# Messages split into a high and a low float32r part, the merge made of float32r products, and a reordered prologue

## The chip, the core and the metric

The kernel runs on one NeuronCore of a Trainium2 chip. The number that counts is the device time of one execution, in microseconds (us). The kernel before has a median of 1049.14 us over three runs (1049.01 to 1050.68).

## The reference

One GNN layer over N = 50000 nodes of D = 128 features and E = 25000 edges, sorted by destination:

```
h    = relu(layernorm(x))                       # without scale and shift
xn   = layernorm(h, g1, b1)
msg  = relu(xn[src] + edge_attr)                # 25000 x 128
aggr = segment_sum(msg, dst, num_segments=N)
z    = (1 + eps_gin) * xn + aggr
x2   = h + relu(z @ Wg1 + bg1) @ Wg2 + bg2
out  = x + x2 + gelu(layernorm(x2, g2, b2) @ Wf1 + bf1) @ Wf2 + bf2      # Wf1: 128 x 512
```

All tensors are float32.

## The kernel before, in words

**Tiles.** Nodes are worked on in 98 blocks of 512 rows (128 partitions x J = 4 rows of 128), edges in 49 chunks of 512 (the same shape). Every engine has its own program, and each walks through the same software pipeline by calling a `step(node, edge, halves, apart)` function; `node(o)` and `edge(o)` give the block or chunk that entered the pipeline o steps ago. With the sorted edges of this input all go through `edges_beside_nodes` (L98 in the profile's numbering): 105 node steps t = 0 to 104, and beside them one chunk every two steps. A chunk's step has two halves: odd t does half 0, even t half 1. Ahead of that, in the prologue, `first_chunks` runs three whole edge steps with no nodes beside them, and `half_chunk` the first half of a fourth (so chunk 3 enters there, and chunk 0 is three steps old). Inside a step the order of instructions of each engine is written out by hand; engines wait for each other on semaphores.

**A chunk's way.** GpSimd (POOL) gathers the source rows of x by indirect DMA into `e_x` (L436). VectorE (DVE) takes statistics (`stats`, L675), ScalarE (ACT) makes `e_relu` (L611), DVE takes its statistics, POOL the power -1/2 of the variance (L501, or, from the fifth chunk on, in one instruction with a node's, L456). DVE scales (`e_zg`, L770), adds b1 to the attributes (`add_b1`, L746) and makes `e_sum` (L792). ACT takes the relu, `e_msg` (L581). Where rows of one partition share a destination they are merged with matmuls: DVE compares destinations into `e_match` (L730, four instructions), and TensorE (PE) multiplies `e_match` with `e_msg` into `p_merged` (L938), six float32 products of 128 columns a chunk.
**A block's way.** DVE: statistics, `n_zg` (L831), `n_in` (L848: needs POOL's power `n_rstd`, L456, and the sums `n_aggr` that SyncE's queue reads back), `n_x2` (L802, opens a step), the out-seed `p_out` (L839), `n_z2T_low` (L689), `n_out` (L826). PE: transposes `p_in` (L927) and `p_z2` (L905), `p_g` (L897), `p_gout` (L912), the first feed-forward product `p_f` (L883) and the second `p_out` (L920).
**Order in the steps that the change touches.** DVE, odd t: `n_x2`, node statistics, `n_out`, `n_zg`, `p_out` seed, `n_in`, then `first_half` (chunk statistics, relu statistics, the small e_ columns, `z2_low`, the four `e_match`, `variance_of`), then `add_b1`. DVE, even t: the same node work, then `second_half` (chunk relu statistics, `e_zg`, `e_index`, `z2_low`, `variance_of`, `e_sum`). PE merges a chunk at the end of odd steps, behind `p_in`. In the prologue POOL does, per step, the power of the chunk two steps old, then the gathers of the new one. ACT does `merged_rows` of chunk 0 in step t = 0.

Of the kernel before, what the change touches and what calls it, by code (L numbers as in the profile page):

```python
# [5 lines left out]
ALU = mybir.AluOpType  # L6
# [4 lines left out]
F32R = mybir.dt.float32r  # L11
BF16 = mybir.dt.bfloat16

P = 128
J = 4
# [96 lines left out]
def gnn_kernel(nc, x, edge_attr, edge_cols, dst_rows, g1, b1, g2, b2, eps_gin,  # L112
# [25 lines left out]
    with ExitStack() as ctx:  # L138
# [9 lines left out]
        def ring_sems(name, depth):  # L148
# [37 lines left out]
        e_x, e_attr, e_relu, e_zg, e_attrb, e_sum, e_msg, e_merged = (  # L186
            sb(f"e_{n}", [P, 3, J, D]) for n in ("x", "attr", "relu", "zg", "attrb", "sum", "msg", "merged"))
# [4 lines left out]
        e_match = sb("e_match", [P, 3, J // PAIR, PAIR * (PAIR + 1) // 2, P])  # L192
# [32 lines left out]
         s_ezg, s_eattrb, s_esum, s_emsg, s_ematch, s_eextra, s_eindex, s_emm, s_emerged) = (  # L225
            sem(f"s_e{n}") for n in (
                "copy", "stat", "minus", "relu", "var0", "statu", "var", "rstd",
                "zg", "attrb", "sum", "msg", "match", "extra", "index", "mm", "merged"))
# [42 lines left out]
        def joined(c, apart):  # L271

            return not apart and c.k >= FIRST_JOINED

# [132 lines left out]
        def _(pool):  # L407
# [51 lines left out]

            def merged_first(edge, apart):  # L460
# [16 lines left out]
            def step(node, edge, halves, apart):  # L477
# [20 lines left out]
                if 0 in halves and (c := edge(2)) is not None and not joined(c, apart):  # L498
                    r, s = c.rows, c.slot(3)
                    pool.wait_ge(s_evar, c.at + 1)  # L500
                    nc.gpsimd.tensor_tensor(e_rstd[0:r, s], e_var[0:r, s, 1], minus_half[0:r, 0:J],  # L501
                                            ALU.pow).then_inc(s_erstd, 1)
                if 0 in halves and (c := edge(0)) is not None:
                    gather(c, range(0, PAIR))
                if 1 in halves and 0 in halves:
                    merged_first(edge, apart)
# [8 lines left out]
        def _(act):  # L515
# [34 lines left out]
            def step(node, edge, halves, apart):  # L550
# [14 lines left out]
                if 1 in halves and 0 not in halves:  # L565
                    merged_rows(edge(3))
# [11 lines left out]
                if 0 in halves and (c := edge(3)) is not None:  # L578
                    act.wait_ge(s_esum, c.at + 1)
                    reached(act, s_emm, c.at - 2)  # L580
                    nc.scalar.activation(e_msg[0:c.rows, c.slot(3)], e_sum[0:c.rows, c.slot(3)],  # L581
# [6 lines left out]
                if 0 in halves and 1 in halves:  # L588
                    merged_rows(edge(3))
# [11 lines left out]
                if (b := node(2)) is not None:  # L601
# [3 lines left out]
                                         ACT.Identity).then_inc(s_inT, 1)  # L605
                if 0 in halves and (c := edge(1)) is not None:
# [18 lines left out]
        def _(dve):  # L625
# [80 lines left out]
            def first_half(c, node):  # L706
# [6 lines left out]
                if c is not None:  # L713
# [5 lines left out]
                                            ALU.mult, ALU.add).then_inc(s_evar0, 1)  # L719
                z2_low(node)  # L720
# [15 lines left out]
                variance_of(node)  # L736

# [258 lines left out]
```

## Time and profile before

| | |
|---|---|
| median of three runs | 1049.14 us |
| the profiled execution: its time, its span | 1047.92 us, 1046.2 us |
| mean granted TensorE clock | 0.984 of full |
| busy share PE / PEld / DVE / ACT / POOL | 94 / 82 / 92 / 82 / 79 % |
| DMA | 156.87 MB, mean 150 GB/s |

Busy time is the union of the instructions' intervals; two instructions that follow each other overlap in it (the next starts before the last one's recorded end), so what an instruction costs on a full engine is the distance from its start to the next start, which is shorter than its duration. The three fullest engines are close together, so the question in every stretch is which one sets the pace.

### The profile page before, as it was taken

Reading aid. Unit: us, or ns where it says so; the run is one execution under the profiler, and the core shown is the slowest. Engines: PE = TensorE matmul, PEld = TensorE weight load, DVE = VectorE, ACT = ScalarE, POOL = GpSimd, SP = SyncE. Lnnn points to the kernel's source line nnn. Section 1 sums busy time; section 2 is a strip of 40 time slices with the busy share of each in tenths; the row PEclk is TensorE's granted clock in tenths of the full one; section 3 lists DMA queues with packets and bytes.
Section 4 is the critical chain, followed back from the end, with each engine's and each line's share of the span. In section 5 each row is a group of like instructions: output and inputs, shape, how many; then the busy total and the mean of one; then the engine's idle time right before and its main releaser. Section 6 shows DMA issues by size and latency. Waiting matters only on the chain. (4 is left out here: it accounts for less than half of the span.)

```text
span 1046.2 us, 23086 instructions
## 1 busy us (share of the span) xinstructions
PE 978.5 (94%) x6684; PEld 853.8 (82%) x6684; DVE 965.6 (92%) x3499; ACT 853.2 (82%) x2158; POOL 823.1 (79%) x510
## 2 busy tenths in 40 slices
PE   0359999999999999999999999999999999999978
PEld 0347888888889888888888888888888888888867
DVE  5789999999999999999999999999999999998732
ACT  1358988988888988888888888888888888988853
POOL 6788888888788888888888888888888888876610
PEclk9679999999999999999999999999999999999999
DMA  7765766877785654565565555554564554443221
GB/s 258 211 180 129 217 171 179 240 227 237 233 254 158 152 138 116 138 142 124 136 146 126 139 142 125 139 144 123 139 146 122 139 146 120 116 112 80 52 60 41
DMA packets 110468, 156.87 MB, mean 150 GB/s; under 512 B 24835, under 2 KB 50607, under 8 KB 110334
## 3 DMA queue, kind: packets, MB, share of 16 engines
q1 hardware_dynamic: 70358, 128.99, 38.9%
q0 software_dynamic: 37760, 25.66, 17.5%
q8 instruction: 56, 0.92, 0.4%
q10 hardware_dynamic: 2216, 0.66, 0.3%
q14 instruction: 78, 0.64, 0.2%
HBM read 90.61 MB, written 64.61 MB: 148 GB/s over the span
## 5 line engine op out<-in xcount | busy, mean ns | idle before, releaser
L447 POOL DMA_INDIRECT aggr_sums<-e_merged,e_index x196 | 337.8, 1724 | 81.4 <-issue 71.9
L920 PE MATMUL p_out<-wf,n_act 128*128 128x128 f32 x3136 | 370.4, 276 | 1.8 <-DVE p_out L839 0.2
L920 PEld LDWEIGHTS p_out<-wf,n_act 128*128 128x128 f32 x3136 | 357.7, 191 | 7.1 <-DVE p_out L839 6.2
L456 POOL TENSOR_TENSOR n_rstd<-n_var,minus_half 128x16 f32<-128x16 f32 (+3 forms) x102 | 259.3, 2554 | 52.6 <-DVE n_var L819 32.1
L522 ACT ACTIVATE n_act<-p_f,bf1e_col 128x512 f32<-128x512 f32 x392 | 256.2, 680 | 35.4 <-PE p_f L883 28.9
L436 POOL DMA_INDIRECT e_x<-in_x,e_cols x196 | 222.0, 1133 | 60.2 <-issue 59.2
L883 PE MATMUL p_f<-n_z2T_high,wf_low 128*128 128x512 f32 x392 | 203.3, 519 | 5.7 <-DVE n_z2T_low L689 5.3
L883 PE MATMUL p_f<-n_z2T_high,wf_high 128*128 128x512 f32 x392 | 155.4, 397 | 0.0
L883 PE MATMUL p_f<-n_z2T_low,wf_high 128*128 128x512 f32 x392 | 155.0, 395 | 0.0
L675 DVE BATCH_NORM_STATS2 n_stat<-n_x 128x6 f32<-128x256 f32 x392 | 140.1, 417 | 0.1
L604 ACT ACTIVATE n_inT<-p_in 128x512 f32<-128x512 f32 x98 | 58.5, 597 | 99.5 <-PE p_in L927 87.5
L848 DVE SCALAR_TENSOR_TENSOR n_in<-n_zg,n_rstd,n_aggr 128x128 f32<-128x128 f32 x392 | 111.2, 344 | 24.2 <-DMA n_aggr<-aggr_sums 18.7
L536 ACT ACTIVATE p_gout<-n_relu,n_rstd 128x128 f32<-128x128 f32 x392 | 128.9, 366 | 4.8 <-DVE n_x L802 3.8
L572 ACT ACTIVATE n_relu<-n_x,n_minus 128x128 f32<-128x128 f32 x392 | 124.7, 397 | 8.7 <-DVE n_minus L813 4.6
L598 ACT ACTIVATE n_z<-n_x,n_rstd 128x128 f32<-128x128 f32 x392 | 125.7, 408 | 4.1 <-POOL n_rstd L456 4.1
L883 PEld LDWEIGHTS p_f<-n_z2T_high,wf_low 128*128 128x128 f32 x392 | 74.4, 190 | 50.3 <-ACT n_act L522 22.2
L912 PE MATMUL p_gout<-wg,n_gT 128*128 128x128 f32 (+1 forms) x784 | 106.8, 280 | 8.7 <-ACT p_gout L536 8.7
L831 DVE SCALAR_TENSOR_TENSOR n_zg<-n_relu,n_stat,g1e_row 128x128 f32<-128x128 f32 x392 | 110.4, 341 | 0.0
L912 PEld LDWEIGHTS p_gout<-wg,n_gT 128*128 128x128 f32 (+1 forms) x784 | 96.5, 193 | 11.7 <-ACT n_gT L530 11.3
L897 PE MATMUL p_g<-n_inT,wg 128*128 128x512 f32 x196 | 101.1, 597 | 1.6 <-ACT n_inT L604 1.6
L938 PE MATMUL p_merged<-e_msg,e_match 128*128 128x128 f32 (+1 forms) x588 | 76.6, 282 | 23.4 <-ACT e_msg L581 17.0
L883 PEld LDWEIGHTS p_f<-n_z2T_low,wf_high 128*128 128x128 f32 x392 | 74.8, 191 | 27.1 <-issue 22.5
(85 smaller groups left out, 1446.0 us busy)
## 6 DMA issues: line engine op xcount, KB each, us to landing
n_x<-in_x SPq DMA_DIRECT2D x97, 256.0 KB
n_aggr<-aggr_sums SPq DMA_DIRECT2D x97, 256.0 KB, 2.7
out_dram<-n_out SPq DMA_DIRECT2D x97, 256.0 KB
aggr_sums<-zeros SPq DMA_DIRECT2D x26, 512.0 KB, 5.2
e_dst<-in_dst_rows SPq DMA_DIRECT2D x49, 256.0 KB
e_attr<-in_attr SPq DMA_DIRECT2D x48, 256.0 KB
aggr_sums<-zeros SPq DMA_DIRECT2D x12, 1024.0 KB
e_x<-in_x,e_cols POOLq DMA_INDIRECT x196
```

What stands on the lines that cost most here:

```text
L436: nc.gpsimd.indirect_dma_start(out=e_x[0:r, s, j, :], out_offset=None, in_=x, in_offset=bass.IndirectOffsetOnAxis(ap=e_cols[0:r, s, 0, j:j ...
L447: nc.gpsimd.indirect_dma_start(out=aggr, out_offset=bass.IndirectOffsetOnAxis(ap=e_index[0:r, s, j:j + 1], axis=0), in_=e_merged[0:r, s, j ...
L456: return nc.gpsimd.tensor_tensor(n_rstd[0:r, s, lo:hi], n_var[0:r, s, lo:hi], minus_half[0:r, 0:(hi - lo) * J].rearrange("p (a j) -> p a j ...
L522: nc.scalar.activation(n_act[:, k, :, 0:b.rows], p_f[k % 2][:, :, 0:b.rows], ACT.Gelu, bias=bf1e_col[:, k:k + 1]).then_inc(s_act, 1)
L536: last = nc.scalar.activation(p_gout[0:r, j, :], n_relu[0:r, b.slot(4), j, :], ACT.Identity, scale=n_rstd[0:r, b.slot(8), 0, j:j + 1])
L572: last = nc.scalar.activation(n_relu[0:r, b.slot(4), j, :], n_x[0:r, b.slot(8), j, :], ACT.Relu, bias=n_minus[0:r, b.slot(8), j:j + 1])
L598: last = nc.scalar.activation(n_z2[0:r, b.slot(2), j, :], n_x2[0:r, b.slot(4), j, :], ACT.Identity, scale=n_rstd[0:r, after_three(b), 2, j ...
L675: last = nc.vector.bn_stats(to[0:rows, j:j + 2, :].rearrange("p j k -> p (j k)"), of[0:rows, j:j + 2, :].rearrange("p j d -> p d j"))
L848: last = nc.vector.scalar_tensor_tensor(n_in[0:r, b.slot(2), j, :], n_zg[0:r, b.slot(2), j, :], n_rstd[0:r, s, 1, j:j + 1], n_aggr[0:r, b. ...
L883: last = nc.tensor.matmul(p_f[k % 2][:, :, 0:b.rows], weights[:, k * P:(k + 1) * P], z2T[:, b.slot(2), :, 0:b.rows], start=(i == 0), stop= ...
L912: last = nc.tensor.matmul(p_gout[0:b.rows, j, :], n_gT[:, b.slot(2), j, 0:b.rows], wg2[:], start=False, stop=True, skip_group_check=True)
L920: last = nc.tensor.matmul(p_out[0:b.rows, j, :], n_act[:, k, j, 0:b.rows], wf2[:, k, :], start=False, stop=(k == KF - 1), skip_group_check ...
```

## The change

It does four things. The messages are kept twice, `e_msg_high` (the relu, written by ACT as float32r, in the place of `e_msg`) and `e_msg_low` (`max(e_sum, 0) - e_msg_high`, a new 128x512 instruction of DVE, `message_low`, with two SBUF inputs, also float32r). `e_match` (zeros and ones) is written as float32r, and each of the six products of a chunk becomes two float32r products, low and high, in the same accumulation. PE waits for the low part. In the prologue (`alone`: no node beside) POOL does a chunk's power between the two pairs of gathers and not ahead of them; DVE adds b1 one step earlier and makes `e_sum` at the start of the step and not at its end; ACT copies chunk 0's merged rows in the half chunk and not in step t = 0. In the steps beside nodes `message_low` stands in `first_half`, behind the small e_ columns and ahead of `z2_low` and `e_match`.

```diff
--- before.py
+++ after.py
@@ -183,13 +183,14 @@
         o_flag = sb("o_flag", [1, 1], I32)
 
 
-        e_x, e_attr, e_relu, e_zg, e_attrb, e_sum, e_msg, e_merged = (
-            sb(f"e_{n}", [P, 3, J, D]) for n in ("x", "attr", "relu", "zg", "attrb", "sum", "msg", "merged"))
+        e_x, e_attr, e_relu, e_zg, e_attrb, e_sum, e_merged = (
+            sb(f"e_{n}", [P, 3, J, D]) for n in ("x", "attr", "relu", "zg", "attrb", "sum", "merged"))
+        e_msg_high, e_msg_low = (sb(f"e_msg_{n}", [P, 3, J, D], F32R) for n in ("high", "low"))
         e_cols = sb("e_cols", [P, 3, 2, J], I32)
         e_dst = sb("e_dst", [P, 3, BLOCK], I32)
         e_dstf, e_count, e_extra = (sb(f"e_{n}", [P, 3, J]) for n in ("dstf", "count", "extra"))
         e_minus = sb("e_minus", [P, 3, J])
-        e_match = sb("e_match", [P, 3, J // PAIR, PAIR * (PAIR + 1) // 2, P])
+        e_match = sb("e_match", [P, 3, J // PAIR, PAIR * (PAIR + 1) // 2, P], F32R)
         e_index = sb("e_index", [P, 3, J], I32)
         e_stat = sb("e_stat", [P, 3, 2, J, 3])
         e_var = sb("e_var", [P, 3, 2, J])
...
@@ -271,6 +272,10 @@
         def joined(c, apart):
 
             return not apart and c.k >= FIRST_JOINED
+
+        def alone(node, apart):
+
+            return node is nothing and not apart
 
         def block_beside(c):
 
@@ -457,6 +462,13 @@
                                                minus_half[0:r, 0:(hi - lo) * J].rearrange("p (a j) -> p a j", j=J),
                                                ALU.pow)
 
+            def power_of_chunk(edge, apart):
+                if (c := edge(2)) is not None and not joined(c, apart):
+                    r, s = c.rows, c.slot(3)
+                    pool.wait_ge(s_evar, c.at + 1)
+                    nc.gpsimd.tensor_tensor(e_rstd[0:r, s], e_var[0:r, s, 1], minus_half[0:r, 0:J],
+                                            ALU.pow).then_inc(s_erstd, 1)
+
             def merged_first(edge, apart):
                 if (c := edge(3)) is not None:
                     r, s = c.rows, c.slot(3)
@@ -495,13 +507,12 @@
                 if 0 in halves and (c := edge(4)) is not None:
                     pool.wait_ge(q_scatter[c.slot(3)], SCATTERED * c.uses(3) + PAIR_SCATTERED)
                     scatter_pair(c, 1)
-                if 0 in halves and (c := edge(2)) is not None and not joined(c, apart):
-                    r, s = c.rows, c.slot(3)
-                    pool.wait_ge(s_evar, c.at + 1)
-                    nc.gpsimd.tensor_tensor(e_rstd[0:r, s], e_var[0:r, s, 1], minus_half[0:r, 0:J],
-                                            ALU.pow).then_inc(s_erstd, 1)
+                if 0 in halves and not alone(node, apart):
+                    power_of_chunk(edge, apart)
                 if 0 in halves and (c := edge(0)) is not None:
                     gather(c, range(0, PAIR))
+                if 0 in halves and alone(node, apart):
+                    power_of_chunk(edge, apart)
                 if 1 in halves and 0 in halves:
                     merged_first(edge, apart)
                 if 1 in halves and (c := edge(0)) is not None:
@@ -562,8 +573,8 @@
                 if (b := node(3)) is not None:
                     hidden(b)
                     seed_gout(b, (2, 3))
-                if 1 in halves and 0 not in halves:
-                    merged_rows(edge(3))
+                if 1 in halves and 0 not in halves and (c := edge(3)) is not None and not c.is_number(0):
+                    merged_rows(c)
                 if (b := node(0)) is not None:
                     r = b.rows
                     act.wait_ge(s_nminus, b.at + 1)
@@ -578,15 +589,15 @@
                 if 0 in halves and (c := edge(3)) is not None:
                     act.wait_ge(s_esum, c.at + 1)
                     reached(act, s_emm, c.at - 2)
-                    nc.scalar.activation(e_msg[0:c.rows, c.slot(3)], e_sum[0:c.rows, c.slot(3)],
+                    nc.scalar.activation(e_msg_high[0:c.rows, c.slot(3)], e_sum[0:c.rows, c.slot(3)],
                                          ACT.Relu).then_inc(s_emsg, 1)
                 if (b := node(5)) is not None:
                     act.wait_ge(s_tz2, b.at + 1)
                     reached(act, s_f, (b.at - 1) * KF)
                     nc.scalar.activation(n_z2T_high[:, b.slot(2), :, 0:b.rows], p_z2[:, :, 0:b.rows],
                                          ACT.Identity).then_inc(s_z2T, 1)
-                if 0 in halves and 1 in halves:
-                    merged_rows(edge(3))
+                if 0 in halves and 1 in halves and (c := edge(3)) is not None and not c.is_number(0):
+                    merged_rows(c)
                 if (b := node(4)) is not None:
                     r = b.rows
                     if b.fixed and b.k >= NB - 4:
@@ -603,6 +614,8 @@
                     reached(act, s_g, b.at - 1)
                     nc.scalar.activation(n_inT[:, b.slot(2), :, 0:b.rows], p_in[:, :, 0:b.rows],
                                          ACT.Identity).then_inc(s_inT, 1)
+                if 0 in halves and (c := edge(3)) is not None and c.is_number(0):
+                    merged_rows(c)
                 if 0 in halves and (c := edge(1)) is not None:
                     r, s = c.rows, c.slot(3)
                     act.wait_ge(s_eminus, c.at + 1)
@@ -703,7 +716,7 @@
                     nc.vector.scalar_tensor_tensor(n_var[0:r, s, 1], n_var[0:r, s, 0], EPS * D,
                                                    n_stat[0:r, s, 1, :, 2], ALU.mult, ALU.add).then_inc(s_nvar, 1)
 
-            def first_half(c, node):
+            def first_half(c, ending, node):
 
                 if c is not None:
                     s, r = c.slot(3), c.rows
@@ -717,6 +730,7 @@
                                             ALU.mult).then_inc(s_eminus, 1)
                     nc.vector.tensor_scalar(e_var[0:r, s, 0], e_stat[0:r, s, 0, :, 2], EPS / D, EPS * EPS,
                                             ALU.mult, ALU.add).then_inc(s_evar0, 1)
+                message_low(ending)
                 z2_low(node)
                 if c is not None:
 
@@ -734,6 +748,15 @@
                                 accum_out=e_count[0:r, s, a:a + 1])
                     last.then_inc(s_ematch, 1)
                 variance_of(node)
+
+            def message_low(c):
+
+                if c is not None:
+                    r, s = c.rows, c.slot(3)
+                    dve.wait_ge(s_emsg, c.at + 1)
+                    reached(dve, s_emm, c.at - 2)
+                    nc.vector.scalar_tensor_tensor(e_msg_low[0:r, s], e_sum[0:r, s], 0.0, e_msg_high[0:r, s],
+                                                   ALU.max, ALU.subtract).then_inc(s_emsg_low, 1)
 
             def add_b1(c):
 
@@ -777,6 +800,10 @@
                                             ALU.max).then_inc(s_eindex, 1)
                 z2_low(node)
                 variance_of(node)
+                sum_of(ending, apart)
+
+            def sum_of(ending, apart):
+
                 if ending is not None:
                     s, r = ending.slot(3), ending.rows
                     if joined(ending, apart):
@@ -849,12 +876,17 @@
                                                               n_rstd[0:r, s, 1, j:j + 1], n_aggr[0:r, b.slot(4), j, :],
                                                               ALU.mult, ALU.add)
                     last.then_inc(s_nin, 1)
+                if alone(node, apart) and 1 in halves:
+                    add_b1(edge(1))
+                    sum_of(edge(2), apart)
+                if alone(node, apart) and 0 in halves:
+                    message_low(edge(3))
                 if 0 in halves or not halves:
-                    first_half(edge(1), node)
-                    if 0 in halves:
+                    first_half(edge(1), None if alone(node, apart) else edge(3), node)
+                    if 0 in halves and not alone(node, apart):
                         add_b1(edge(2))
                 if 1 in halves:
-                    second_half(edge(1), edge(2), node, apart)
+                    second_half(edge(1), None if alone(node, apart) else edge(2), node, apart)
                 if (b := first) is not None and b.is_number(1):
                     finish_parameters()
 
@@ -930,14 +962,16 @@
                 if 0 in halves and (c := edge(3)) is not None:
                     s, r = c.slot(3), c.rows
                     pe.wait_ge(s_ematch, c.at + 1)
-                    pe.wait_ge(s_emsg, c.at + 1)
+                    pe.wait_ge(s_emsg_low, c.at + 1)
                     reached(pe, s_emerged, c.at)
                     for g in range(J // PAIR):
                         for i in range(PAIR):
                             for a in range(i + 1):
-                                last = nc.tensor.matmul(p_merged[0:r, g * PAIR + i, :],
-                                                        e_match[0:r, s, g, match_at(a) + i - a, 0:r],
-                                                        e_msg[0:r, s, g * PAIR + a, :], start=(a == 0), stop=(a == i))
+                                for part, msg in enumerate((e_msg_low, e_msg_high)):
+                                    last = nc.tensor.matmul(p_merged[0:r, g * PAIR + i, :],
+                                                            e_match[0:r, s, g, match_at(a) + i - a, 0:r],
+                                                            msg[0:r, s, g * PAIR + a, :],
+                                                            start=(a == 0 and part == 0), stop=(a == i and part == 1))
                     last.then_inc(s_emm, 1)
 
             half_chunk(step)
```

(The lines left out add the semaphore `s_emsg_low`.)

## Rows read from the trace of the kernel before

**Rows 1.** The page: busy time, share of the span and instructions of each engine.
```profile
PE 978.5 (94%) x6684; PEld 853.8 (82%) x6684; DVE 965.6 (92%) x3499; ACT 853.2 (82%) x2158; POOL 823.1 (79%) x510
```

**Rows 2.** The chain that ended last, in order of time: start us, us, what.
```profile
945.08 0.62 DVE p_out L839
...
945.75 3.84 PE p_out L920 x32
...
951.36 1.39 PE p_f L883 x6
...
969.34 1.31 PE p_merged L938 x12
970.65 0.71 PE p_f L883 x3
```

**Rows 3.** Timeline of DVE: start, us, line, tile; L802 opens a step.
```profile
92.57 0.67 DVE L802 TENSOR_TENSOR n_x<-p_gout,rows 128x512 f32<-128x512 f32 x1
...
102.19 0.67 DVE L802 TENSOR_TENSOR n_x<-p_gout,rows 128x512 f32<-128x512 f32 x1
...
111.98 0.68 DVE L802 TENSOR_TENSOR n_x<-p_gout,rows 128x512 f32<-128x512 f32 x1
...
931.43 0.68 DVE L802 TENSOR_TENSOR n_x<-p_gout,rows 128x512 f32<-128x512 f32 x1
```

**Rows 4.** Waits of DVE from 92 to 931: us in total, times, longest.
```profile
DVE n_in L848 <- DMA n_aggr<-aggr_sums: 5.2, 8, 1.2
DVE n_in L848 <- POOL n_rstd L456: 4.8, 6, 2.2
```

**Rows 5.** Timeline of POOL, two steps from 500 us.
```profile
500.84 2.32 POOL L456 TENSOR_TENSOR n_rstd<-n_var,minus_half 128x12 f32<-128x12 f32 x1
503.79 1.65 POOL L447 DMA_INDIRECT aggr_sums<-e_merged,e_index  x1 [0.63 <-issue]
...
520.41 2.31 POOL L456 TENSOR_TENSOR n_rstd<-n_var,minus_half 128x12 f32<-128x12 f32 x1
```

**Rows 6.** Timeline of DVE, end of an odd step.
```profile
515.11 0.68 DVE L689 TENSOR_TENSOR n_z2T_low<-p_z,n_z2T_high 128x512 fp32r<-128x512 f32 x1
...
517.14 0.68 DVE L746 TENSOR_TENSOR e_attrb<-e_attr,rows 128x512 f32<-128x512 f32 x1
517.74 0.68 DVE L802 TENSOR_TENSOR n_x<-p_gout,rows 128x512 f32<-128x512 f32 x1
```

**Rows 7.** Timeline of ACT in the same step.
```profile
513.63 0.63 ACT L581 ACTIVATE e_msg<-e_sum 128x512 f32<-128x512 f32 x1
```

**Rows 8.** Timeline of DVE in the prologue, a one-input instruction of 512 columns.
```profile
25.80 0.48 DVE L652 TENSOR_SCALAR wf1g<-wf,g_col 128x512 f32<-128x512 f32 x1
...
26.19 0.28 DVE L653 TENSOR_SCALAR g1e_row<-rows,eps_col 128x128 f32<-128x128 f32 x1
```

**Rows 9.** Timeline of PE, the last block: its shorter products and transposes.
```profile
1032.14 0.46 PE L905 MATMUL p_z<-ident,n_z 84*128 84x84 f32 x4
...
1032.43 3.77 PE L920 MATMUL p_out<-wf,n_act 128*128 128x128 f32 x32
...
1036.21 0.32 PE L883 MATMUL p_f<-n_z2T_low,wf_high 128*128 128x336 f32 x1
...
1036.83 0.31 PE L883 MATMUL p_f<-n_z2T_high,wf_high 128*128 128x336 f32 x1
```

**Rows 10.** Timeline of all engines, prologue and first steps.
```profile
17.93 1.08 POOL L501 TENSOR_TENSOR e_rstd<-e_var,minus_half 128x4 f32<-128x4 f32 x1 [4.02 <-DVE e_var L764]
...
30.50 0.57 ACT L547 ACTIVATE e_merged<-p_merged 128x512 f32<-128x512 f32 x1
...
31.95 1.63 POOL L447 DMA_INDIRECT aggr_sums<-e_merged,e_index  x1 [3.40 <-ACT e_merged L547]
...
60.71 0.76 DVE L675 BATCH_NORM_STATS2 e_stat<-e_x 128x6 f32<-128x256 f32 x2 [2.15 <-DMA e_x<-in_x,e_cols]
...
78.70 0.76 DVE L675 BATCH_NORM_STATS2 e_stat<-e_x 128x6 f32<-128x256 f32 x2 [2.05 <-DMA e_x<-in_x,e_cols]
```

More of the change, by code:

```diff
@@ L224, in gnn_kernel @@
         (s_ecopy, s_estat, s_eminus, s_erelu, s_evar0, s_estatu, s_evar, s_erstd,
-         s_ezg, s_eattrb, s_esum, s_emsg, s_ematch, s_eextra, s_eindex, s_emm, s_emerged) = (
+         s_ezg, s_eattrb, s_esum, s_emsg, s_emsg_low, s_ematch, s_eextra, s_eindex, s_emm, s_emerged) = (
             sem(f"s_e{n}") for n in (
                 "copy", "stat", "minus", "relu", "var0", "statu", "var", "rstd",
-                "zg", "attrb", "sum", "msg", "match", "extra", "index", "mm", "merged"))
+                "zg", "attrb", "sum", "msg", "msg_low", "match", "extra", "index", "mm", "merged"))
         q_x, q_aggr, q_out = ring_sems("q_x", 8), ring_sems("q_aggr", 4), ring_sems("q_out", 2)
```

## The prediction

> **What bounds the kernel now.** The page's first part shows three engines near full, PE 94%, DVE 92%, POOL 79% plus what it spends between its DMA instructions [rows 1]. Shares don't tell which of them sets the pace, so I read the chain of waits next. Up to 945 us it lies on DVE alone, back to back; there PE's `p_out` is released by DVE's seed of it, and from then on, when the chunks have run out on DVE, the chain is PE back to back until the last merge at 969 us [rows 2]. Then I took DVE's timeline, where `n_x` (L802) opens each step. An odd step (first half of a chunk) takes 9.62 us (92.57 to 102.19), an even one 9.79 us (102.19 to 111.98) [rows 3]. These two are DVE's own work, 19.41 us a pair: I went through all the steps, and the 43 odd ones from t = 7 to 91 are within 0.1 us of 9.62 but for two of 9.97, while the even ones have 9.77 as their floor and are often 0.2 to 1.3 us above it, once 2.3. From t = 7 to t = 92 it is 931.43 - 92.57 = 838.9 us, against 43 x 9.62 + 42 x 9.79 = 824.8: so 14 us are waits, nearly all in even steps. The waits of DVE name 10 of them: `n_in` waits for sums read back from DRAM (5.2) and for POOL's power (4.8) [rows 4], that is, for POOL's queue to run late.
>
> The other two have little room. PE's pair, read where PE is the chain, is from `p_f` at 951.36 to `p_f` at 970.65, 19.29 us [rows 2]. POOL's is 520.41 - 500.84 = 19.57 with about 0.4 us of waiting in it (a 0.63 us idle before a scatter, of which 0.2 us stand before every first scatter), so about 19.1 us [rows 5]. DVE sets the pace, the others follow 1 to 2% behind.
>
> **The change, part by part.**
>
> *The low part on DVE.* One instruction of 128x512 with two SBUF inputs for each of 49 chunks. The nearest row is `e_attrb` (L746): same shape, two SBUF inputs; it starts at 517.14 and the next starts at 517.74, so it costs 0.60 us of a full DVE, although its duration is 0.68 [rows 6]. That `z2_low`, which writes float32r, has the same 0.68 says that the output type costs nothing. The lower bound is a one-input instruction of 512 columns, 26.19 - 25.80 = 0.39 us [rows 8], the upper one the full duration, 0.68. I take 0.60. It adds no wait for its input: ACT's `e_msg` ends at 514.26, and the new instruction would start at 515.11, where `z2_low` starts now [rows 6, 7]. What is queued behind it (`z2_low`, `e_match`, `variance_of`) shifts by 0.60, with its consumers a step later. It stands in each odd step; chunks 4 to 46 meet it in the stretch from t = 7 to 91: 43 x 0.60 = +25.8 us, with nothing of DVE's taken away in exchange. (The type of `e_match` changes, its four instructions stay.)
>
> *What the waits give back.* The even steps' 14 us come from POOL and its DMAs being late, with 0.3 us a pair of room (19.41 against 19.1). A pair of 20.01 us gives POOL three times that room, so a late scatter or gather is caught up sooner. If all vanish, 14 us come back, if nothing changes, none. I take waits in inverse proportion to the room, a third left, so -9 us.
>
> *The merge on PE.* Six float32 products give way to twelve float32r ones. Before, 12 records take 1.31 us (969.34 to 970.65), 0.11 each [rows 2]. The cost of a float32r record goes by its columns: at 512, 1.39 / 6 = 0.232 us [rows 2], at 336, (1036.83 - 1036.21) / 4 = 0.155 [rows 9]. That is columns / 2.4 GHz plus 0.015 to 0.019 us, which at 128 columns gives 0.07 us, or 0.84 us a chunk: 0.5 us less on PE. No row has a float32r product of 128 columns. The bounds are the 0.07 of that line and 0.232, if a narrow product cost as a full one. On the path this counts only where PE is the chain, behind t = 93, for the merges of the last two chunks: -1.0 us. Everywhere else PE only waits longer for DVE's seed of `p_out`.
>
> One thing could forbid even that gain: each of the twelve has its own weight load of 128 columns. The transposes of the last block load 128 columns each and follow each other every (1032.43 - 1032.14) / 4 = 0.07 us [rows 9], so a load need not take more than that beside the stream. The Trainium skill says otherwise (TensorE: Matmul & The Clock Gate, LDWEIGHTS): a load takes its number of columns divided by 1.2 GHz, 107 ns for 128 whatever the rows. By that rule, twelve loads would hold the merge at 1.28 us, PE would gain nothing, and the forecast would be 1 us higher; the trace's 0.07 disagrees with it.
>
> *The prologue.* POOL idles 4.02 us before the first power [rows 10]; the change lets the first pair of chunk 2's gathers run in it. What counts later is when POOL can begin with the scatter of chunk 0, since from 31.95 us POOL runs almost without a pause, and DVE's next waits (2.15 us at 60.71, 2.05 at 78.70) are for its gathers [rows 10]. I went through the order by hand: `e_sum` of chunk 0 comes 4 us earlier, at about 20.6; the low part is made behind the parameters, at 26.5 to 27.1 (a new dependence: before, PE needed only the relu); twelve products at the low clock take 1.3 to 1.6 us, and `e_merged` starts at about 28.7 instead of 30.50. So POOL starts some 1.8 us sooner. The `message_low` of t = 1, 3 and 5 fall into waits for gathers, but part of the last reaches t = 7: I take -1.2 us, between -4 (if the earlier gathers also shorten the later waits) and +0.6.
>
> **The sum**, on the profiled execution: 1047.92 - 1.2 + 25.8 - 9 - 1.0 = 1062.5 us. The median of the runs is 1.2 us above the profiled one, so 1063.7.
>
> **The rivals.**
>
> *A, the waits give nothing back.* They are then DMA latencies that move along with the steps. For it: a part is put down to the read-back of `n_aggr`, not to POOL. Against: floor steps exist between them. 1047.92 - 1.2 + 25.8 - 1.0 = 1071.5, with the offset 1073.
>
> *B, a narrow float32r product costs no less than a float32 one* (two records each, or four passes at few columns), so twice as many products cost twice as much: 2.6 us a chunk (2.8 at 0.232 each). For it: no row excludes it, the narrowest float32r row has 336 columns. Against: the line through 512 and 336 columns. PE's pair becomes 19.29 + 1.31 = 20.6 us, more than DVE's 20.0, and sets the pace: 42.5 pairs x 20.6 = 875.5 against 838.9, +36.6, and +2.6 for the last two merges: 1047.92 - 1.2 + 36.6 + 2.6 = 1086, with the offset 1087.
>
> *C, not slower: DVE is not the pacer, POOL is.* Then the place to look is the wait before `n_in`; the new instruction fills it. The price that it can hide is the whole 14 us; with 2 us from prologue and last merges, the kernel is not slower once the instruction costs less than 16 / 43 = 0.37 us, just below the 0.39 of the one-input row. For it: POOL is 98% taken. Against: 43 odd steps at the floor show a DVE without any wait, and two inputs have cost 0.60. It gives 1049.
>
> **How the numbers follow.** Forecast 0.68, A 0.13, B 0.11, C 0.05, something else 0.03. Predicted is the forecast, 1063.7. Its own range is 1057 (waits all gone, -4 in the prologue) to 1070 (a third of the waits given back, 0.62 us an instruction). The 8 in 10 range takes in A and part of what lies between it and B: 1056 to 1078. About 0.2% (2 us) is what can be told from no change. Slower: forecast, A, B and most of the rest, 0.93; within: 0.04; faster: 0.03.
>
> **What would show it.** In the trace after: odd steps of DVE of 10.22 us, even ones still 9.79 at the floor, with fewer above it; `message_low` at 0.60 from start to start, 49 of them. PE idle of 0.5 us or more a pair before `p_out`, released by DVE, and a merge of 0.84 us in 12 records. Waits of `n_in` under 10 us. First scatter at about 30 us. It is wrong if the odd steps grow by less than 0.5 us (then the cost of the instruction is off), if the chain lies on PE in the middle of the run (B), or if the waits in even steps stay at 14 us (A) or take the new work in whole (C).

## The result, and the profile after

The changed kernel has a median of 1069.4 us (1067.95 to 1070.24, four runs) against 1049.91 of the kernel before beside it: 1.0173 times the time, 95% interval 1.0154 to 1.0191. Slower, as forecast (1063.7), by 19.5 us where 14.6 had been expected, and inside the range.

The changed kernel's page, busy time, answers to [rows 1]:

```profile
PE 1001.5 (94%) x6684; PEld 859.4 (81%) x6684; DVE 992.5 (93%) x3548; ACT 856.9 (80%) x2158; POOL 830.5 (78%) x510
```

DVE has 49 instructions and 27 us more, PE the same number of records. Its timeline in the changed kernel, the starts of steps (L829 is what L802 was), beside [rows 3]:

```profile
96.00 0.68 DVE L829 TENSOR_TENSOR n_x<-p_gout,rows 128x512 f32<-128x512 f32 x1
106.27 0.68 DVE L829 TENSOR_TENSOR n_x<-p_gout,rows 128x512 f32<-128x512 f32 x1
116.03 0.68 DVE L829 TENSOR_TENSOR n_x<-p_gout,rows 128x512 f32<-128x512 f32 x1
...
950.39 0.68 DVE L829 TENSOR_TENSOR n_x<-p_gout,rows 128x512 f32<-128x512 f32 x1
```

An odd step now takes 10.27 us (median of the 43: 10.24, floor 10.21), an even one 9.76 (median 9.77, where it was 9.92). Summed up by these starts, both profiled executions divide like this:

| stretch | before | after | difference | forecast |
|---|---|---|---|---|
| start of the span to t = 7 | 92.6 | 96.0 | +3.4 | -1.2 |
| 43 odd steps, t = 7 to 91 | 414.5 | 442.2 | +27.7 | +25.8 |
| 42 even steps, t = 8 to 90 | 424.3 | 412.2 | -12.1 | -9 |
| t = 92 to the end of the span | 114.8 | 115.8 | +1.0 | -1.0 |
| span | 1046.2 | 1066.2 | +20.0 | +14.6 |

The two middle rows are the change as forecast, with one thing that the rows hide. The first 41 odd steps grew by 25.1 us, 0.61 each; the last two, at 10.56 and 11.63 us, hold 1.4 us of waits more, where before the last even step had held its longest (12.05). Counted against the floors of both kinds of steps (9.61 and 9.77 before, 10.21 and 9.76 now), 15.3 us of waits have become 5.4. The new instruction in the changed kernel's timeline, in its place ahead of `z2_low`, costs 0.61 us from start to start, as its neighbours of the same shape do (0.60 to 0.61):

```profile
524.24 0.69 DVE L758 SCALAR_TENSOR_TENSOR e_msg_low<-e_sum,e_msg_high 128x512 fp32r<-128x512 f32 x1
524.85 0.69 DVE L702 TENSOR_TENSOR n_z2T_low<-p_z,n_z2T_high 128x512 fp32r<-128x512 f32 x1
```

And POOL, which ran late before, now waits for DVE. Its waits in the changed kernel from 96 to 950 us:

```profile
POOL n_rstd L461 <- DVE n_var L846: 26.3, 42, 0.7
POOL aggr_sums L452 <- DVE n_var L787: 11.0, 36, 0.3
```

The second of these is named so for 2.4 us before, the first for none. DVE's waits for `n_in` are down from the 10 us of [rows 4] to 1.3. One of the announced signs came out smaller: PE's weight loads for `p_out` wait for DVE's seed 42 times, 12.3 us in all, 0.3 us a pair of steps and not 0.5 or more.

Three parts came out otherwise. The merge on PE has hardly become cheaper. In the changed kernel's chain (which beside [rows 2] is PE again from the last release by DVE on) the twelve products take 1.29 us where 0.84 was forecast:

```profile
964.75 3.84 PE p_out L952 x32
...
969.03 1.29 PE p_merged L971 x12
970.32 1.45 PE p_f L915 x6
```

The part behind t = 92 is 1.0 us longer where 1.0 less was forecast. In the chains the two last merges take 1.29 and 1.09 us against 1.34 and 1.31, 0.3 less together. What is lost lies behind the wait for the last sums: from `p_in` to `p_out` the chain takes 8.2 us (1021.23 to 1029.43) against 7.1 (1002.54 to 1009.64), and the mean granted clock there is 0.67 against 0.77. What moved the clock there was not looked into.

And the start is late. In the timeline of PE and DVE of the changed kernel, between 60 and 84 us:

```profile
60.23 0.76 DVE L688 BATCH_NORM_STATS2 e_stat<-e_x 128x6 f32<-128x256 f32 x2 [2.42 <-DMA e_x<-in_x,e_cols]
61.77 0.68 DVE L758 SCALAR_TENSOR_TENSOR e_msg_low<-e_sum,e_msg_high 128x512 fp32r<-128x512 f32 x1
62.55 0.45 PE L971 MATMUL p_merged<-e_msg_low,e_match 128*128 128x128 f32 x1 [3.25 <-issue]
80.99 0.76 DVE L688 BATCH_NORM_STATS2 e_stat<-e_x 128x6 f32<-128x256 f32 x2 [3.44 <-DMA e_x<-in_x,e_cols]
82.53 0.69 DVE L758 SCALAR_TENSOR_TENSOR e_msg_low<-e_sum,e_msg_high 128x512 fp32r<-128x512 f32 x1
83.32 0.45 PE L971 MATMUL p_merged<-e_msg_low,e_match 128*128 128x128 f32 x1 [4.47 <-issue]
```

DVE waits for gathered rows of a new chunk; the low part of an older chunk stands behind that wait in its queue; PE waits for the low part (3.25 and 4.47 us), and behind PE's merge stand all its other products. Between 96 and 950 us DVE waits for gathered rows once, 1.3 us, so there the order costs little.

### The profile page after: what moved, and what is told of

It reads as the page before. It is cut to its first block and busy times, and to the rows that moved or that the text cites. A ratio compares the mean times of both kernels' runs of the same rounds, so it can differ in the third digit from the quotient of the medians.

```text
span 1066.2 us, 23180 instructions
## 1 busy us (share of the span) xinstructions
PE 1001.5 (94%) x6684; PEld 859.4 (81%) x6684; DVE 992.5 (93%) x3548; ACT 856.9 (80%) x2158; POOL 830.5 (78%) x510
## 5 line engine op out<-in xcount | busy, mean ns | idle before, releaser
L441 POOL DMA_INDIRECT e_x<-in_x,e_cols x196 | 228.3, 1165 | 62.0 <-issue 58.1
L915 PE MATMUL p_f<-n_z2T_high,wf_low 128*128 128x512 f32 x392 | 206.3, 526 | 1.6 <-DVE n_z2T_low L702 1.2
L944 PE MATMUL p_gout<-wg,n_gT 128*128 128x128 f32 (+1 forms) x784 | 109.2, 283 | 3.7 <-ACT p_gout L547 3.7
L929 PE MATMUL p_g<-n_inT,wg 128*128 128x512 f32 x196 | 103.7, 611 | 1.4 <-ACT n_inT L615 1.4
L971 PE MATMUL p_merged<-e_msg_low,e_match 128*128 128x128 f32 (+1 forms) x294 | 73.9, 291 | 32.0 <-DVE e_msg_low L758 16.8
```

Source lines behind the costliest of these rows:

```text
L441: nc.gpsimd.indirect_dma_start(out=e_x[0:r, s, j, :], out_offset=None, in_=x, in_offset=bass.IndirectOffsetOnAxis(ap=e_cols[0:r, s, 0, j:j ...
L915: last = nc.tensor.matmul(p_f[k % 2][:, :, 0:b.rows], weights[:, k * P:(k + 1) * P], z2T[:, b.slot(2), :, 0:b.rows], start=(i == 0), stop= ...
L944: last = nc.tensor.matmul(p_gout[0:b.rows, j, :], n_gT[:, b.slot(2), j, 0:b.rows], wg2[:], start=False, stop=True, skip_group_check=True)
```

## The experiments

All ran on the chip beside the kernel before, whose median there was 1050.4 to 1051.5 us. "t = 7" is the start of that step on DVE in the profile, "middle" the stretch from there to t = 92 (before 92.6 and 838.9, changed kernel 96.0 and 854.4). Each kernel has one profile, and the executions of one kernel differ by 2 to 7 us, so a difference of 1 or 2 us between two profiles shows little unless the medians or other rows say the same.

**The new prologue alone** (no low part, merge in float32 as before):

```diff
-                                for part, msg in enumerate((e_msg_low, e_msg_high)):
-                                    last = nc.tensor.matmul(...)
+                                last = nc.tensor.matmul(..., e_msg[...], start=(a == 0), stop=(a == i))
...
-                    nc.vector.scalar_tensor_tensor(e_msg_low[0:r, s], ...)
```

> The kernel before with the reordered prologue alone: float32 merge, no low part. Theory: the new order is a small gain (in the changed kernel POOL's first scatter starts at 31.0 us instead of 31.95), and the 3.4 us that the changed kernel is late at step t = 7 come from the low part. So about 1 us below the kernel before, 1049 us, and t = 7 starts at 91.5 to 92.5 us. Rival: the reordering itself costs the 4 us; then 1054 and t = 7 at about 96.

Measured: 1045.6 us, ratio 0.9946 (0.9927 to 0.9964). t = 7 at 88.7, middle 837.8. The new order gains more than I thought: 3.9 us at t = 7. The first merge starts at 23.38 us:

```profile
23.38 2.90 PE L966 MATMUL p_merged<-e_msg,e_match 128*128 128x128 f32 x12 [13.47 <-ACT e_msg L591]
```

So the low part costs the start 7.3 us (96.0 against 88.7), not 3.4; the gain of the prologue hid half of it. The medians agree: the two kernels are 23.8 us apart, of which the middle has 16.6 and the part behind t = 92 nothing.

**The change with the old prologue:**

```diff
         def alone(node, apart):
-            return node is nothing and not apart
+            return False
...
-                if 0 in halves and (c := edge(3)) is not None and c.is_number(0):
-                    merged_rows(c)
```

> The changed kernel with the old order of the prologue. Theory: about 1 us more than the changed kernel, 1070 to 1071, t = 7 again at 96 or later. Rival (the reordering costs the time): 1065, t = 7 at 92 to 93.

Measured: 1071.55 us, ratio 1.0179 (1.0157 to 1.0201), 2.2 us over the changed kernel; t = 7 at 101.7, middle 854.4. The rival (1065) is out. The profile shows 5.7 us more at t = 7, but the ratio can't be told from the changed kernel's 1.0173 (1.0154 to 1.0191), since the kernel before was 1.1 us slower beside this run. The sign is the theory's in the profile alone, and the size stays open.

**The low part of chunks 1 to 3 ahead of the gather wait:**

```diff
             def first_half(c, ending, node):
+                early = ending is not None and ending.fixed and ending.k <= 3
+                if early:
+                    message_low(ending)
...
-                message_low(ending)
+                if not early:
+                    message_low(ending)
```

> The changed kernel with the low part of chunks 1 to 3 made ahead of the chunk statistics, so that it does not stand behind DVE's wait for gathered rows. Theory: PE's waits of 3.25 us (at 62.55) and 4.47 us (at 83.32) before the merge go, the granted clock rises at about 65 us as before and not at 88, and t = 7 starts 3 us sooner: 1066 us. Rival (the lateness comes from DMA landing or from DVE's added 0.6 us each): 1069, t = 7 at 95.5 to 96.

Measured: 1065.9 us, ratio 1.0133 (1.0111 to 1.0155), t = 7 at 93.5. As the theory has it, 3.5 us less in the medians (2.5 at t = 7, where 3 was expected), and PE's merge follows its `p_in` at 58.06 us without a wait. The clock is less tidy. The granted clock (the third number from the right) in ten-microsecond stretches, first of the kernel before, then of the changed kernel, then of this one:

```profile
60.00:70.00 10.00, 5.30 (x27) 4.10 (x25) 9.29 (x39) 6.33 (x19) 8.14 (x7) 0.84 0.71 208
70.00:80.00 10.00, 4.69 (x30) 3.57 (x30) 7.95 (x32) 6.13 (x19) 8.86 (x6) 0.98 0.50 136
```

```profile
60.00:70.00 10.00, 6.03 (x21) 4.52 (x22) 9.16 (x36) 4.75 (x14) 7.40 (x6) 0.50 0.69 182
70.00:80.00 10.00, 7.31 (x25) 4.99 (x24) 7.41 (x30) 6.80 (x21) 8.86 (x6) 0.50 0.51 139
```

```profile
60.00:70.00 10.00, 3.87 (x15) 2.67 (x14) 9.78 (x41) 6.11 (x19) 7.35 (x6) 0.79 0.61 177
70.00:80.00 10.00, 8.25 (x30) 6.58 (x30) 6.95 (x26) 6.13 (x17) 8.85 (x6) 0.50 0.59 133
```

At 0.50 TensorE runs at 1.2 GHz. It came up sooner here, but fell back from 70 us on, so "the clock rises as before" was half right, and what it is worth by itself was not separated. The changed kernel stays at 0.50 or 0.51 through both stretches.

**In addition chunk 0's low part as soon as its high part is there:**

```diff
+                    if alone(node, apart) and c.is_number(1):
+                        message_low(EDGES.at_step(0)(0))
                     for j in range(J):
                         last = nc.vector.scalar_tensor_tensor(e_zg...
```

> As the kernel that makes the low part of chunks 1 to 3 early (1065.9), and chunk 0's low part is made as soon as its high part is there, inside the second half of the prologue's last whole step and not behind the parameters. Theory: the first merge starts at about 24.1 us instead of 26.5, the first scatter at about 28.5 instead of 30.8, and everything up to t = 7 is 1.5 to 2.3 us sooner: 1064. Rival (the scatters are not what the start waits for): 1066.

Measured: 1060.95 us, ratio 1.0105 (1.0083 to 1.0126), t = 7 at 89.9. More than expected: 5 us below the last one, with the first merge at 24.83 us and the first scatter at 29.2 (28.5 expected). With the low part taken off both queues' heads the start is 1.3 us behind that of the prologue alone, and so is the first scatter (29.2 against 27.8). So most of the 7.3 us comes from where the instruction stands, not from its 0.6 us.

**The low part computed twice:**

```diff
-                    nc.vector.scalar_tensor_tensor(e_msg_low[0:r, s], ...).then_inc(s_emsg_low, 1)
+                    for to in (e_again, e_msg_low):
+                        last = nc.vector.scalar_tensor_tensor(to[0:r, s], ...)
+                    last.then_inc(s_emsg_low, 1)
```

> The changed kernel with the low part computed twice (the first result goes to a tile that nobody reads). Theory: DVE sets the pace and nearly no waits are left to give back: odd steps grow by another 0.60 us, 43 x 0.60 = 26 us, and 1 to 2 us come off the 2.3 us of waits left: 1094 us. Rival (each instruction is hidden by half in waits, as the 17.3 us for 43 steps of the first could also be read: 19.5 / 43 = 0.45 each): 1089.

Measured: 1096.6 us, ratio 1.0428 (1.0406 to 1.0449), 27.2 over the changed kernel; odd steps 10.83 (median), together 467.2 us, +25.0; even ones 411.9, as before the doubling; t = 7 2.6 us later. The second instruction costs its 0.6 us in the odd steps and nothing more comes back: the time is 2.6 us over the 1094 expected, about what the start lost. The rival (0.45 each, 1089) falls.

**The new instruction in the kernel before, its result unread:**

```diff
+                message_low(ending)          # reads e_sum and e_msg, writes e_msg_low; PE waits for s_emsg as before
                 z2_low(node)
```

> The kernel before (old prologue, float32 merge) with the new DVE instruction in its place, its result read by nobody, so that PE does not wait for it. Theory: the middle costs the same as in the change (27.7 us for 43 instructions less 12 us of waits, about +15.5), and at the start nothing is queued behind it: t = 7 starts at most 2 us later than the 92.6 of before. Together 1065 to 1067, against 1071.5 with PE waiting for it. Rival (the loss at the start is DVE's time, or the lower clock of a lighter merge): t = 7 at 99 to 101 and 1071.

Measured: 1067.6 us, ratio 1.0166 (1.014 to 1.0192); t = 7 at 95.3, middle 857.0 (+18.2). Between the theories at the start: 2.8 us later than before with nobody waiting for the instruction, 6.3 us sooner than with PE waiting for it (101.7). The time, 0.6 us above the 1065 to 1067 expected, is the theory's, not the rival's 1071. So with the old prologue about a third of the 9.1 us comes with DVE's instruction itself and two thirds with PE's wait for it and the new merge.

**High part alone** (the low part of the messages is left out of the merge; six float32r products a chunk, no new DVE instruction, new prologue):

```diff
-                                for part, msg in enumerate((e_msg_low, e_msg_high)):
+                                for part, msg in enumerate((e_msg_high,)):
```

> The changed kernel without the low part: no DVE instruction for it and six float32r products a chunk instead of twelve. It leaves out the low part of the messages from the merge. Theory: DVE is the pacer and the merge on PE is worth nothing in the middle, although it falls to 6 x 0.111 = 0.67 us: odd steps 9.62, even ones with the 11 us of waits that the kernel with the new prologue alone has (1045.6), and 1.3 us less behind the last chunks: 1044 to 1045. Rival (PE paces together with DVE, and its time causes the waits of the even steps): 1035 to 1038.

Measured: 1039.0 us, ratio 0.9891 (0.9869 to 0.9913). Between theory and rival in the medians, 6.6 us below the prologue alone; in the profiles the middle is 835.2 against 837.8 and the part behind t = 92 2.3 us shorter, while t = 7 is 1.5 us later. The waits of the even steps are nearly the same (10.8 us above the floor against 11.0), so PE's merge does not cause them, and of the 2.6 us in the middle 2.2 are DVE's waits for gathered rows (0.2 against 2.4). But PE was given 0.6 us less a chunk and the medians fell by 6.6 us, of which the profiles show 3.4 (this one is of its kernel's slowest execution, that of the prologue alone of its fastest). The part of the rival that concerns the even steps is out; how much of the 6.6 us comes from PE pacing together with DVE stays open. Six products are expected at 0.67 us and take 0.70 (510.43 to 511.13).

**Products of 64 columns**, twice as many with the same weights:

```diff
-                            for a in range(i + 1):
+                            for lo in (0, D // 2):
+                                for a in range(i + 1):
...
+                                                                msg[0:r, s, g * PAIR + a, lo:lo + D // 2],
```

> The changed kernel with each product of the merge cut into two of 64 columns, so 24 products with the same stationary operand of 128 columns. Theory (the weight load sets the 0.111 us of a product): 24 x 0.107 to 0.111 = 2.6 to 2.7 us a chunk, PE's pair 20.6 us against DVE's 20.0, PE becomes the pacer in the middle: about +22 us and +2.6 behind, 1092 to 1095. Rival (the stream sets it): 24 products of 0.03 to 0.07 us, at most 1.7 us a chunk, no change: 1069 to 1070.

Measured: 1104.0 us, ratio 1.0516 (1.0486 to 1.0547), 34.6 us over the changed kernel and 9 above the theory's range: t = 7 is 8.3 us later (the first merge alone takes 5.11 us, 26.69 to 31.80, at the slow spacing), which the theory had left out, the middle 25.8 us longer where 22 was expected. The time misses; what decides between theory and rival is the spacing of the products. Its timeline of PE:

```profile
506.15 0.28 PE L972 MATMUL p_merged<-e_msg_low,e_match 128*128 128x64 f32 x1
506.26 0.28 PE L972 MATMUL p_merged<-e_msg_high,e_match 128*128 128x64 f32 x1
...
508.72 0.28 PE L972 MATMUL p_merged<-e_msg_high,e_match 128*128 128x64 f32 x1
508.83 0.48 PE L915 MATMUL p_f<-n_z2T_high,wf_low 128*128 128x512 f32 x1
```

24 products of 64 columns in 2.68 us are 0.112 us each, the same as for 128 columns: the length of the stream plays no part, what goes with the weights does. DVE's pair of steps from 497.50 to 518.16 is 20.66 us, what rival B had computed for PE (20.6), so here PE sets the pace. In the changed kernel's own trace the last chunk says it too. There the weights have 106 rows and 106 columns and the stream still 128, and a product takes (989.19 - 988.26) / 10 = 0.093 us:

```profile
988.26 0.26 PE L971 MATMUL p_merged<-e_msg_high,e_match 106*106 106x128 f32 x1
...
989.19 0.26 PE L971 MATMUL p_merged<-e_msg_high,e_match 106*106 106x128 f32 x1
```

The Trainium skill's rule (TensorE: Matmul & The Clock Gate, LDWEIGHTS), columns divided by 1.2 GHz, gives 107 and 88 ns; the runs agree to 5 ns, and I had weighed it wrongly. That it is the columns and not the rows no product here separates.

**The sign changes of the means on ACT** (on top of the new prologue alone), a test in the other direction, work taken from DVE:

```diff
-                    nc.vector.tensor_scalar(n_minus[0:r, s], n_stat[0:r, s, 0, :, 1], -1.0, None, ALU.mult)
+                    nc.scalar.activation(n_minus[...], n_stat[0:r, s, 0, :, 1], ACT.Identity, scale=-1.0)
```

(and `e_minus` likewise)

> The kernel with the new prologue alone (1045.6), with the two small sign changes of the means (128x4 each, one per node step, one per chunk) made by ACT and not by DVE. Theory: DVE is the pacer, each of these costs it 0.065 us from start to start, so a pair of steps falls from 19.41 by 0.2 us; 42.5 x 0.2 = 8.4 us less, of which POOL (19.1 us a pair) takes part back as waits of the even steps: 3 to 6 us less, 1040 to 1043. Rival (the pace is shared so evenly that nothing moves, or ACT's two more instructions delay PE): 1045 or more.

Measured: 1046.9 us, ratio 0.9953 (0.9935 to 0.9972). No gain, as the rival had it. The middle is 837.1 against 837.8. Odd steps have a floor of 9.54 but a median of 9.72, so that the floors add up to 19.30 a pair, PE's own, and the medians to 19.51. In the two runs below, which share one edit, the median is 9.72 again with the float32 merge and 9.55 with six float32r products in its place: so it is PE's merge that holds the odd steps back here. t = 7 is 4.3 us later, a loss at the start that was not taken apart.

**The same from block 8 and chunk 5 on**, once with the float32 merge, once with the high part alone (which leaves out the low part of the messages):

```diff
+        def late(item, first):
+            return item.fixed and item.k >= first
...
+                    if not late(b, 8):
                         nc.vector.tensor_scalar(n_minus[...
```

> The kernel with the new prologue alone (1045.6), with the sign changes of the means made by ACT from block 8 and chunk 5 on, so that the start is untouched. Theory: PE with its float32 merge stands right behind DVE; when all of them were moved, a pair of steps went from 19.39 only to 19.51 in the middle, so DVE's 0.2 us a pair bring nothing: 1044.5 to 1046. Rival (the loss of the first version was all at the start, and DVE alone paces the middle): 1040 to 1042.

> The kernel with float32r products of the high part alone (1039.0; the low part of the messages is left out of the merge), with the same late sign changes on ACT. Theory: with 0.67 us less on PE, DVE is the pacer with room behind it on PE, and POOL (19.1 us a pair) is next: 0.1 to 0.2 us a pair of DVE's 0.2 come through, 3 to 6 us less, 1033 to 1036. Rival (POOL's lateness already takes all, as the waits of the even steps grow by what DVE loses): 1038.5 to 1039.5.

Measured: 1043.45 us, ratio 0.9937 (0.9916 to 0.9957), and 1039.3 us, 0.9901 (0.9871 to 0.9931). The first is between its two expectations (middle 834.9), and its ratio can't be told from that of the prologue alone; the second meets its rival in the medians (1039.0 without the edit), although its middle fell by 4.4 us to 830.8 in the profile while start and end lost 2.5. Whether DVE's 0.2 us a pair can be turned into time once PE is relieved stays open.

## Why the prediction was right, and where not

**The pacer.** Right. "DVE sets the pace, the others follow 1 to 2% behind" was read from the floor of the odd steps, and the runs that make an engine's work longer agree: +0.6 us a chunk for the first and the second new instruction on DVE, PE in front at 20.66 us once its pair is made longer. The runs that make it lighter say that the margin over PE, 0.1 us a pair, is too thin to call DVE the only pacer before the change: lighter DVE work brought little, and a lighter merge on PE brought 6.6 us in the medians.

**The new instruction.** 0.60 taken, 0.60 to 0.61 measured from start to start. Of the 27.7 us, against 25.8 for the 43, the rest is waits in the last two steps.

**What the waits give back.** The mechanism was right (POOL late, then POOL waiting). In the even steps all but 2.3 of 14 us went, more than the forecast 9; counted over both kinds of steps it is 9.9 of 15.3, about the two thirds forecast, though the inverse proportion to the room that gave them is not shown by one pair of kernels. The doubled instruction, with more room still, gave nothing further back.

**The merge on PE.** Wrong: "at 128 columns gives 0.07 us". The line through 512 and 336 columns is the cost of the stream; at 128 columns the weight load is longer and takes its place: 0.111 us a product, 1.29 in place of 0.84 for the twelve. The 0.07 us, which I set against 0.107, was the wrong row. It is from the last block, whose transposes have weights of 84 rows and a stream of 84 columns. The transposes of a full block, in the same trace of the kernel before, follow each other every (502.62 - 502.19) / 4 = 0.108 us:

```profile
502.19 0.60 PE L905 MATMUL p_z<-ident,n_z 128*128 128x128 f32 x4
502.62 1.06 PE L912 MATMUL p_gout<-wg,n_gT 128*128 128x128 f32 x8
```

Why those of the last block are quicker was not separated.

It cost 0.7 us of the forecast behind t = 92 (0.3 saved of 1.0). Had the merge been on the path, it would have cost 0.5 us a chunk.

**The prologue.** The step that failed: "The `message_low` of t = 1, 3 and 5 fall into waits for gathers". They stand behind these waits, not in them, and PE, whose merge had needed nothing that DVE makes behind that wait, waits with them. And of chunk 0's low part I named the new dependence, but put its twelve products at 1.3 to 1.6 us; they took 2.49 (26.68 to 29.17), and the first scatter came at 31.01 us, not at about 30. I did not ask what the new order would give without the low part (first merge at 23.38). The -1.2 was 1.8 us of an earlier scatter less 0.6 for what reaches t = 7. Measured it is +3.4: a gain of 3.9 and a loss of 7.3, and the low part in its best place brings the loss down to 1.3.

**Rivals.** A (nothing given back) fell, its number (1073) was nearer by chance. B's mechanism exists in another form: a narrow float32r product costs half of a float32 one, so twelve cost what six did, not twice as much. C fell with the result itself, 19.5 us slower where it gave none, and again with the doubled instruction.

**The sum.** By the table, the profiled execution is 5.4 us over the forecast: 4.6 at the start, 2.0 behind t = 92, and 1.2 under it in the middle. The forecast's own range, redone from its terms, runs from 1056 to 1069 (1071 with +0.6 at the start) and not from 1057 to 1070, so the 1069.4 lies at its upper end, moved there by the start.

**What beats both.** Of the versions that compute the same, the new prologue alone, 1045.6 us, and 1043.45 with the late sign changes on ACT, two that can't be told apart by their ratios. The split itself is a loss in this kernel in every place tried: 1060.95 at best.

## What to carry to other kernels

Read the pacer from the floor of single steps and not from busy shares, and count what it waits for beside it: lengthening the pacer's work gave two thirds of those waits back here, and then no more. When a product's operand gets a second producer, ask for every stage of the pipeline, the start above all, what the new instruction is queued behind on its engine, since the consumer inherits that wait with all that stands behind it. A price read from a stretch of other sizes has to be checked against a full-size row before it is used. With 128 columns of weights and 128 of stream, splitting a float32 product into two float32r ones saved nothing here: two records of 0.11 us either way.

## What the runs showed of the hardware

A float32r product with 128 columns of weights starts 0.111 to 0.112 us after the one before at the full clock, whether its stream has 128 or 64 columns; with 106 rows and columns of weights it is 0.093 us. At 1.2 GHz it is 0.214 us (changed kernel, 62.79 to 64.93, ten gaps, granted clock 0.50). The clock can rise within one merge, and the spacing goes with it. In the run with the low part of chunks 1 to 3 early, the granted clock is 0.50 up to 58.9 us and 0.98 from 59 to 60, and the products of one merge are first 0.22 and then 0.11 us apart:

```profile
58.52 0.41 PE L975 MATMUL p_merged<-e_msg_low,e_match 128*128 128x128 f32 x1
58.74 0.41 PE L975 MATMUL p_merged<-e_msg_high,e_match 128*128 128x128 f32 x1
...
59.34 0.27 PE L975 MATMUL p_merged<-e_msg_high,e_match 128*128 128x128 f32 x1
59.45 0.28 PE L975 MATMUL p_merged<-e_msg_low,e_match 128*128 128x128 f32 x1
```

The spacing also shows where the clock's row can't be read: in the first merge of the changed kernel it is 0.213 us ((29.06 - 26.93) / 10), that of 1.2 GHz, while the granted clock from 25 to 30 us stands as 1.00.

A scalar_tensor_tensor of DVE with an immediate and two SBUF inputs of 128x512, output float32r, costs 0.60 to 0.61 us from start to start, the same as a tensor_tensor.
